# Ternary feed-forward: second matrix's ternary weights, centring, lower clip and two batch rows' preparation on GpSimd; batch rows prepared one by one

## The reference

```python
def absmax_quant(x):
    gamma = jnp.max(jnp.abs(x), axis=-1, keepdims=True)
    x_hat = jnp.clip(x * Q_B / gamma, -Q_B + EPS, Q_B - EPS)
    return x_hat * gamma / Q_B
def ternarize_weights(w):
    gamma = jnp.mean(jnp.abs(w))
    return jnp.sign(jnp.round(w / (gamma + EPS))) * gamma
def bitlinear(x, w):
    xn = layer_norm(x)
    x_hat = xn + jax.lax.stop_gradient(absmax_quant(xn) - xn)
    w_hat = w + jax.lax.stop_gradient(ternarize_weights(w) - w)
    return jnp.einsum('bsd,od->bso', x_hat, w_hat)
h = bitlinear(x, w_fc)      # 256 -> 1024
...                         # gelu, then bitlinear(h, w_proj), 1024 -> 256
```

## Time and profile before

| | us |
|---|---|
| median of 3 runs | 1640.0 (1637.98 to 1640.43) |
| the profiled execution, its own time | 1639.1 |
| its span in the trace | 1637.1 |
| the feed-forward stage, first to last instruction | about 276.4 to 344.4 |

### The profile page before, as it was taken

How to read it: one execution, slowest core, us unless ns; L and a number is a source line. 1 busy time by engine, 2 the same in 40 slices (tenths; PEclk the granted TensorE clock), 3 DMA queues, 4 the chain that set the end, 5 groups by cost and what they waited for, 6 DMA issues and landing times. The chain is left out here.

```text
span 1637.1 us, 25648 instructions
## 1 busy us (share of the span) xinstructions
PE 1462.8 (89%) x8204; PEld 847.8 (52%) x8204; DVE 1305.8 (80%) x2612; ACT 1022.6 (62%) x2407; POOL 1133.5 (69%) x1034
## 2 busy tenths in 40 slices
PE   6598697758779999899999999989989999999988
PEld 5477465433444555455455555545545555554455
DVE  7876576878669888888978888888888888888865
ACT  3364464744366877677677767677666766767552
POOL 2364462112458889988878998878899888887742
PEclk9799798879899999999999999999999999999999
DMA  3000841020100001000000000000000000000020
GB/s 103 1 3 2 280 133 39 1 74 0 33 1 14 12 3 35 20 1 1 1 1 1 28 14 1 1 1 1 14 28 1 1 1 1 1 1 0 1 59 27
DMA packets 30974, 38.45 MB, mean 23 GB/s; under 512 B 4980, under 2 KB 26488, under 8 KB 30840
## 3 DMA queue, kind: packets, MB, share of 16 engines
q1 hardware_dynamic: 30840, 36.82, 7.0%
HBM read 35.76 MB, written 1.05 MB: 22 GB/s over the span
## 5 line engine op out<-in xcount | busy, mean ns | idle before, releaser
L2145 POOL TENSOR_TENSOR stream_acc<-stream_acc,stream_weights 128x512 f32<-128x512 f32 (+1 forms) x374 | 491.9, 1315 | 74.2 <-ACT stream_weights L2044 52.3
L1975 PE MATMUL stream_banks<-stream_weights,stream_v 128*128 128x512 f32 (+1 forms) x876 | 450.0, 598 | 0.0
L2038 ACT COPY stream_weights<-stream_banks 128x512 f32<-128x512 f32 (+1 forms) x438 | 255.8, 584 | 226.7 <-PE stream_banks L1950 216.8
L2217 DVE TENSOR_TENSOR stream_most<-stream_most,stream_banks 128x512 bf16<-128x512 bf16 (+1 forms) x416 | 284.7, 684 | 138.4 <-ACT stream_weights L2038 124.0
L2044 ACT ACTIVATE stream_weights<-stream_weights 128x512 f32<-128x512 f32 (+1 forms) x438 | 278.0, 635 | 66.6 <-DVE stream_weights L2203 62.8
L2203 DVE TENSOR_TENSOR stream_weights<-stream_weights,stream_banks 128x512 f32<-128x512 f32 (+1 forms) x438 | 296.8, 680 | 1.9 <-PE stream_banks L1965 0.6
L1950 PE MATMUL stream_banks<-stream_q_t_hi,stream_k_t_hi 128*128 128x512 bf16 (+1 forms) x480 | 183.1, 381 | 15.4 <-DVE stream_most L2217 13.9
L2152 POOL TENSOR_TENSOR stream_by_cos<-stream_by_cos,stream_by_sin 128x256 f32<-128x256 f32 x192 | 135.8, 728 | 79.0 <-DVE stream_by_sin L2263 79.0
L1950 PE MATMUL stream_banks<-stream_q_t_hi,stream_k_t_lo 128*128 128x512 bf16 (+1 forms) x480 | 182.8, 381 | 0.0
L1950 PE MATMUL stream_banks<-stream_q_t_lo,stream_k_t_hi 128*128 128x512 bf16 (+1 forms) x480 | 182.8, 381 | 0.0
L1975 PEld LDWEIGHTS stream_banks<-stream_weights,stream_v 128*128 128x128 f32 (+1 forms) x876 | 145.2, 191 | 29.8 <-issue 4.3
(11 more groups left out here) (443 smaller groups left out, 3097.6 us busy)
## 6 DMA issues: line engine op xcount, KB each, us to landing
memory_raw_t<-in_ctx_t SPq DMA_DIRECT2D x4, 1601.0 KB, 8.9
memory_raw<-in_ctx SPq DMA_DIRECT2D x4, 1536.0 KB
row_ctx_t<-in_ctx_t SPq DMA_DIRECT2D x6, 512.0 KB, 3.6
early_raw<-in_L_xattn_Wq SPq DMA_DIRECT2D x4, 512.0 KB, 3.8
early_raw<-in_L_xattn_Wo SPq DMA_DIRECT2D x4, 512.0 KB, 3.9
row_ctx_t<-in_ctx_t SPq DMA_DIRECT2D x1, 1601.0 KB, 6.9
moe_raw_up<-in_L_ffn_wi SPq DMA_DIRECT2D x6, 256.0 KB, 4.9
model_x<-in_x SPq DMA_DIRECT2D x1, 1024.0 KB, 5.6
```

The costliest lines, as they stand in the source:

```text
L1975: nc.tensor.matmul(ps[:, 2 + n, :], v[0:r, g % 2, t, :], room(step)[0:r], start=(t == 0), stop=(t == KT - 1)).then_inc(weighed, 1)
L2038: nc.scalar.copy(room(step)[0:r], ps[0:r, step % 2, :]).then_inc(copied, 1)
L2145: nc.gpsimd.tensor_tensor(acc[0:r, h % 2, :], acc[0:r, h % 2, :], room(step)[0:r], ALU.add).then_inc(acc_ready, 1)
L2217: nc.vector.tensor_tensor(most[0:r], most[0:r], ps[0:r, step % 2, :], ALU.max).then_inc(maxed, 1)
```

## The change

On GpSimd instead of VectorE: normalising, scaling and clipping of batch rows 2 and 3, the second matrix's two compares and the subtraction, and the lower clip of every hidden tile. On GpSimd instead of ScalarE: the centring of every hidden tile. VectorE prepares rows 0 and 1 one by one, and takes the greatest sizes of rows 2 and 3 one by one. ScalarE's sum of the absolute weights stands behind the high halves of rows 0 and 1, TensorE's spreading of it behind up(0), in PSUM bank 7 instead of 2. The diff, cut to its core:

```diff
 @block.gpsimd
+                def normalise_rows(b):
+                    for t in range(QT * b, QT * (b + 1)):
+                        last = nc.gpsimd.tensor_scalar(rows[:, t, :], x[:, t, :], mean_var[:, t, 0:1], rs[:, 1, t:t + 1],
+                                                       ALU.subtract, ALU.mult)
+                    last.then_inc(rest_normed, 1)
+
+                def scale_rows(b):
+                    gp.wait_ge(rest_sized, b - 1)
+                    for t in range(QT * b, QT * (b + 1)):
+                        last = nc.gpsimd.tensor_scalar(rows[:, t, :], rows[:, t, :], top[:, 1, t:t + 1], CLIP, ALU.mult, ALU.min)
+                    link(last)
+                    some = rows[:, QT * b:QT * (b + 1), :]
+                    nc.gpsimd.tensor_scalar(some, some, -CLIP, None, ALU.max).then_inc(rest_ready, 1)
+
                 def centre(t):
                     gp.wait_ge(h_ready, t + 1)
                     nc.gpsimd.tensor_scalar(hmean[:, t:t + 1], hsum[:, t:t + 1], -1.0 / FF, None, ALU.mult).then_inc(mean_ready, 1)
+                    gp.wait_ge(mean_ready, t + 1)
+                    if t >= 3:
+                        gp.wait_ge(h_t, t - 2)
+                    nc.gpsimd.tensor_scalar(off[:, t % 3, :], h[:, t % 2, :], hmean[:, t:t + 1], None, ALU.add).then_inc(off_ready, 1)
+
+                def clip(t):
+                    part = off[:, t % 3, :]
+                    gp.wait_ge(h_scaled, t + 1)
+                    nc.gpsimd.tensor_scalar(part, part, -CLIP, None, ALU.max).then_inc(h_clipped, 1)
...
+                gp.wait_ge(rs_known, 1)
+                normalise_rows(2)
+                normalise_rows(3)
+                scale_rows(2)
+                scale_rows(3)
+                centre(0)
+                gp.wait_ge(sizes_known, 1)
+                flat = tern[1][:].rearrange("p c n -> p (c n)")
+                nc.gpsimd.tensor_scalar(below[:], raw[:], per_size[:, 0:1], -0.5, ALU.mult, ALU.is_lt)
+                centre(1)
+                clip(0)
+                link(nc.gpsimd.tensor_scalar(flat, raw[:], per_size[:, 0:1], 0.5, ALU.mult, ALU.is_gt))
+                nc.gpsimd.tensor_tensor(flat, flat, below[:], ALU.subtract).then_inc(proj_ready, 1)
                 for t in range(TILES):
-                    centre(t)
-                    if t >= 1:
-                        deviate(t - 1)
-                deviate(TILES - 1)
+                    if t + 2 < TILES:
+                        centre(t + 2)
+                    if t + 1 < TILES:
+                        clip(t + 1)
+                    deviate(t)
 @block.vector
+                normalise_rows(0)
+                link(size_rows(0))
+                scale_rows(0)
+                normalise_rows(1)
+                link(size_rows(1))
+                scale_rows(1)
+                lower_rows(0)
+                for b in range(2, BATCH):
+                    ve.wait_ge(rest_normed, b - 1)
+                    size_rows(b).then_inc(rest_sized, 1)
+                lower_rows(1)
...
-                nc.vector.tensor_scalar(below[:], raw[:], per_size[:, 0:1], -0.5, ALU.mult, ALU.is_lt)
-                link(nc.vector.tensor_scalar(flat, raw[:], per_size[:, 0:1], 0.5, ALU.mult, ALU.is_gt))
-                nc.vector.tensor_tensor(flat, flat, below[:], ALU.subtract).then_inc(proj_ready, 1)
...
-                    link(nc.vector.tensor_scalar(part, part, htop[:, 1, t:t + 1], CLIP, ALU.mult, ALU.min))
-                    nc.vector.tensor_scalar(part, part, -CLIP, None, ALU.max).then_inc(h_clipped, 1)
+                    nc.vector.tensor_scalar(part, part, htop[:, 1, t:t + 1], CLIP, ALU.mult, ALU.min).then_inc(h_scaled, 1)
 @block.scalar
                 high_rows(0)
                 high_rows(1)
+                ac.wait_ge(loaded, 16)
+                nc.scalar.activation(sized[:], raw[:], ACT.Abs, accum_out=size[:]).then_inc(sizes_ready, 1)
                 gelu(0)
-                centre(0)
                 high_rows(2)
                 high_rows(3)
                 square(0)
                 gelu(1)
-                centre(1)
                 square(1)
                 for t in range(TILES):
                     if t + 2 < TILES:
                         gelu(t + 2)
-                        centre(t + 2)
                     high(t)
 @block.tensor
                 turn_rows(0)
                 turn_rows(1)
+                up(0)
                 pe.wait_ge(sizes_ready, 1)
-                nc.tensor.matmul(ps[:, 2, 0:1], ones[:], size[:], start=True, stop=True).then_inc(size_spread, 1)
-                up(0)
-                pe.wait_ge(size_taken, 1)
+                nc.tensor.matmul(ps[:, 7, 0:1], ones[:], size[:], start=True, stop=True).then_inc(size_spread, 1)
                 up(1)
                 turn_rows(2)
                 turn_rows(3)
```

More of the change, by code:

```diff
@@ L913, in ternary_ffn @@
         CLIP = 128.0 - 1e-6
-        HALF_TILES = TILES // 2
         raw = sb("raw_proj", [P, FC * DM])
@@ L947, in ternary_ffn @@
             sem("ones_ready"), sem("sizes_ready"), sem("size_spread"), sem("sizes_known"), sem("size_taken"))
-        proj_ready = sem("proj_ready")
+        proj_ready, pool_step = sem("proj_ready"), sem("pool_step")
+        rs_known, rest_normed, rest_sized, rest_ready, h_scaled = (
+            sem("rs_known"), sem("rest_normed"), sem("rest_sized"), sem("rest_ready"), sem("h_scaled"))
         rows_ready, rows_t, hi_ready, lo_ready = sem("rows_ready"), sem("rows_t"), sem("hi_ready"), sem("lo_ready")
@@ L961, in _ @@
             def _(gp):
+                link = chain(gp, pool_step)
                 nc.gpsimd.memset(half[:], -0.5)
@@ L985, in _ @@
                 ve.wait_ge(rs_done, 1)
-                link(nc.vector.reciprocal(rs[:, 1, :], rs[:, 1, :]))
+                nc.vector.reciprocal(rs[:, 1, :], rs[:, 1, :]).then_inc(rs_known, 1)
+                ve.wait_ge(rs_known, 1)
                 def lower_rows(b):
@@ L992, in lower_rows, with normalise_rows @@
                                             rows_hi[:, :, tok], ALU.subtract).then_inc(lo_ready, 1)
-                for s in range(2):
-                    tiles = range(HALF_TILES * s, HALF_TILES * (s + 1))
-                    some = slice(tiles.start, tiles.stop)
-                    for t in tiles:
+                def normalise_rows(b):
+                    for t in range(QT * b, QT * (b + 1)):
                         last = nc.vector.tensor_scalar(rows[:, t, :], x[:, t, :], mean_var[:, t, 0:1], rs[:, 1, t:t + 1],
@@ L1000, in _, with size_rows, scale_rows @@
                     link(last)
+                def size_rows(b):
+                    some = slice(QT * b, QT * (b + 1))
                     link(nc.vector.tensor_reduce(top[:, 0, some], rows[:, some, :], AX_X, ALU.max, apply_absolute_value=True))
                     nc.vector.tensor_scalar(up_size[:, some], top[:, 0, some], const["fc_mean"][:, 0:1], 1.0 / 128.0, ALU.mult, ALU.mult)
-                    if s == 1:
-                        lower_rows(0)
-                        lower_rows(1)
                     link(nc.vector.reciprocal(top[:, 1, some], top[:, 0, some]))
-                    link(nc.vector.tensor_scalar(top[:, 1, some], top[:, 1, some], 128.0, None, ALU.mult))
-                    for t in tiles:
+                    return nc.vector.tensor_scalar(top[:, 1, some], top[:, 1, some], 128.0, None, ALU.mult)
+                def scale_rows(b):
+                    for t in range(QT * b, QT * (b + 1)):
                         last = nc.vector.tensor_scalar(rows[:, t, :], rows[:, t, :], top[:, 1, t:t + 1], CLIP, ALU.mult, ALU.min)
                     link(last)
-                    nc.vector.tensor_scalar(rows[:, some, :], rows[:, some, :], -CLIP, None, ALU.max).then_inc(rows_ready, 1)
+                    some = rows[:, QT * b:QT * (b + 1), :]
+                    nc.vector.tensor_scalar(some, some, -CLIP, None, ALU.max).then_inc(rows_ready, 1)
+                normalise_rows(0)
[9 more added lines that the diff above has]
+                lower_rows(1)
                 ve.wait_ge(size_spread, 1)
-                nc.vector.tensor_scalar(mean_size[:], ps[:, 2, 0:1], 1.0 / (FF * DM), None, ALU.mult).then_inc(size_taken, 1)
+                nc.vector.tensor_scalar(mean_size[:], ps[:, 7, 0:1], 1.0 / (FF * DM), None, ALU.mult).then_inc(size_taken, 1)
                 ve.wait_ge(size_taken, 1)
@@ L1070, in _ @@
                 nc.scalar.activation(rs[:, 1, :], rs[:, 0, :], ACT.Sqrt).then_inc(rs_done, 1)
-                ac.wait_ge(loaded, 16)
-                nc.scalar.activation(sized[:], raw[:], ACT.Abs, accum_out=size[:]).then_inc(sizes_ready, 1)
                 def high_rows(b):
@@ L1126, in turn_rows @@
                 def turn_rows(b):
-                    pe.wait_ge(rows_ready, b // QT + 1)
+                    if b < 2:
+                        pe.wait_ge(rows_ready, b + 1)
+                    else:
+                        pe.wait_ge(rest_ready, b - 1)
+                    if b == 3:
```

(1 more changed line is left out.)

8 lines of the change are left out of this document (1 added, 7 removed).

## The result

The changed kernel takes 1670.2 us (median of 4 runs, 1666.5 to 1675.1) against 1640.2 before (4 runs, 1638.0 to 1641.4): a ratio of 1.0186 [1.0156, 1.0217]. The prediction was 1638.5 us with a range of 1634 to 1650. The profiled execution took 1666.5 us with a span of 1664.4, 27.3 us over the span of before.

A forecast was written before the change was run, and what follows sets the result against it. VectorE was taken to bound the feed-forward tile loop, TensorE the step before it. Front +3.7 and loop -3.45 gave +0.25 us; with -0.7 for an earlier clock, 1639.1 became 1638.4, stated as 1638.5; range 1634 to 1650.

The forecast's parts named there:

- the price of GpSimd's one-source passes: Moved GpSimd passes: 0.82 ns an element, so 0.42 us for 256 wide, 1.05 for 1024, 1.89 for 2048.
- the upper end of the bounds: Moved one-source GpSimd passes: at most the two-source price, 2.21 ns an element.
- The rival with the two-source price: GpSimd pays 2.2 ns for one-source passes: turn 1 some 13 us late, period 6.2 us, about 1656; chance 0.23.
- The front: Stage before the tile loop: first centring done 1.3 us early, then GpSimd's queue makes turn 1 (second hidden-tile transposes) 3.7 us late.
- The loop: Tile loop, turns 2 to 7: VectorE loses the lower clip, period 5.37 to 4.68 us, 3.45 us gained.
- The subtraction: Second matrix's 16-bit subtraction on GpSimd: 1.96 ns an element, 4.02 us.
- its rival at 1.89: Cheap 16-bit subtraction gives 2.1 us back; with a warm TensorE 1634.5; chance 0.22.
- The port: Shared by wide VectorE scales and GpSimd passes, which take turns; in the loop only the scale exposed, costed at nothing.
- up to 1.05 us a tile: Loop: cost of the scale's wait at the shared port where the centring's cover fails.
- TensorE: Step from turn 1 to turn 2: TensorE's own, mostly at 1.2 GHz, taken again as 6.46 us.
- the sum's term of 1.9 us: Front: full TensorE clock granted sooner brings up(1), transposes and Gelu(1) up to 1.9 us earlier; middle taken, -0.7.
- The warm TensorE of a rival: Turn 1 to turn 2 at the loop's clock, 4.6 instead of 6.46 us; with cheap subtraction 1634.5; chance 0.22.

The follow-up runs named there:

- p1_forms: Kernel before plus thirteen GpSimd passes of 1024 elements at the feed-forward stage's start, VectorE held back, to price operation forms: 1671.4 us in one run.
- p2_pairs: Kernel before plus thirteen more such GpSimd passes, testing order and pairs of operations: max-then-min clip 3.65 us, min-then-max 1.04 us.
- e12: Changed kernel with every move kept but written in cheap operation pairs, weights rounded in three passes: 1634.3 us, ratio to before 0.9970.
- e6: Kernel before with the hidden tiles' lower clip left out on every engine: 1637.7 us, ratio to before 0.9985.
- e5: Changed kernel keeping only row-by-row preparation on VectorE and the later sum of absolute weights: 1636.3 us, ratio to before 0.9983.
- e14: e12 with the second matrix's compares and subtraction back on VectorE: 1632.9 us, ratio to before 0.9951.

## Why the prediction was wrong

**The step that failed is the price of GpSimd's one-source passes.** The prediction took 0.82 ns an element, "the row of the same kind" in the earlier trace rows. That row (L676) multiplies *and* adds two constants, and by p1_forms and p2_pairs this is one of three pairs that are cheap. The moved clip and centring are single operations, at 2.78 us for 1024 elements, the row scales and compares multiply-min and multiply-compare, at 3.65 (the rows' normalising, subtract-multiply at 1.31 us for 256, was not probed by itself). The 1-wide passes of the earlier trace rows cost about 0.21, so 1024 elements cost 2.5 and 3.4 ns each: three and four times the price taken, and above the upper end of the bounds, 2.21 ns, which assumed that no one-source pass is dearer than a two-source one. The row was near in shape and not in operations (its source of bytes is not the reason: 1.05 us from bytes and from floats), and the prediction's own sentence against itself ("min, max and pointer scalars, which no GpSimd row shows") was nearer to the mark; pointers, though, turned out nearly free.

- **The rival with the two-source price** was the mechanism that happened: turn 1 late, then GpSimd the bound of the loop. Its sizes were too small by the same term: turn 1 lies 24.6 us later in the stage (14.5 + 10.1), for the rival's 13, and the period is 7.0, for its 6.2.
- **The front.** By the prediction's own queue, with the measured prices: centring 2.87, compare 7.19, mean 0.66, centring 2.86 and clip 2.77 from 293.97 end at 310.33, where turn 0 starts. Turn 0 to turn 1 is a compare of 7.62, the subtraction of 4.05, mean 0.23, centring 2.86 and clip 2.77, 17.5 us. The queue order was read rightly; each entry was mis-sized. Rows 2 and 3 ended on GpSimd at 293.7 for the same reason, which is 295.0 on the time axis of before (the stage starts 1.3 us earlier in the changed span), instead of near 290. So the centring of tile 0 started 3.6 us later than predicted, though Gelu(0), at 289.16 or 290.4, was within 0.3 us of its forecast.
- **The loop.** VectorE's saving was right as a mechanism: with cheap pairs the period is 4.60 us (e12; 4.68 predicted), and without the clip it falls to 4.65 in the last two steps (e6). Over turns 2 to 7 e6 gains only 2.8 us; that its whole stage is 3.5 us shorter, next to the 3.45 predicted, is chance, since 0.7 of it lies ahead of turn 0. The saving is not seen in the changed kernel, where GpSimd's 6.8 us set the period. Two readings behind it are off without effect: VectorE was idle for 2.4 of the 27 us, of which the 1.5 are the part before the low half, and 0.75 less the overlap of 0.08 is 0.67 us, not 0.70.
- **The subtraction** was right at 4.05, its rival at 1.89 wrong. Two 16-bit sources cost 1.98 ns an element there, no less than the 1.96 ns of the row with 32-bit sources and a 16-bit result.
- **The port** was told rightly and does not make the loss. VectorE's scale of 0.75 us ends 0.55 us after the compare that it meets (304.56, after 304.01), having taken 6.04 us, and the later one is stretched too; timeline of DVE:

```profile
298.52 6.04 DVE L1079 TENSOR_SCALAR ffn_off<-ffn_off,ffn_htop 128x1024 f32<-128x1024 f32 x1
309.27 1.61 DVE L1079 TENSOR_SCALAR ffn_off<-ffn_off,ffn_htop 128x1024 f32<-128x1024 f32 x1
```

  In the front the clip behind it is waiting for GpSimd's queue anyway. A dearer pass also stretches the scale longer, which the prediction's "up to 1.05 us a tile" took from the same price. The compare that the 1-wide pass at 291.77 met is not the one of the earlier trace rows, which ends at 291.47, but the next, timeline of DVE before:

```profile
291.38 1.28 DVE L1022 TENSOR_SCALAR ffn_tern_proj<-ffn_raw_proj,ffn_per_size 128x2048 f16<-128x2048 f32 x1
```

- **TensorE.** The step from turn 1 to turn 2 took 6.9 us, for the 6.5 expected. From turn 0 to turn 1 its mean granted clock is 0.60 (0.83 before), with 5.38 of 17.62 us busy. The full clock did come sooner, as the sum's term of 1.9 us supposed: up's pairs of matmuls fall from 1.06 to about 0.59 us at 13.5 us into the stage (288.69), before at 15.4 (291.85). But GpSimd is then still at the rows, and the lead is gone by turn 0. The warm TensorE of a rival came about in e5, e12 and e14, where the step from turn 1 to turn 2 takes 4.4 us at a granted clock of 1.00; not here, where it is 0.64.

The Trainium skill (GPSIMD Engine Reference, introduction) has VectorE "roughly 2× faster" at such arithmetic, and the prediction set that aside. The runs put the clip at 2.77 against 0.69 us, a factor of 4.0, and as min and max at 1.04, a factor of 1.5: neither is 2, and the measurement decides. The Trainium skill (GPSIMD Engine Reference, Engine selection) calls one-input passes "roughly line-rate"; of the passes measured here only the three pairs, copies and casts come near that, at 1.5 times VectorE's 0.69 us. A compare of 2048 took 7.2 us, about twice the 3.7 that the prediction had worked out from the Trainium skill (GPSIMD Engine Reference, Performance pitfalls for Q7 kernels).

Why just these pairs are cheap was not tried; a reader has the list, not the reason.
